# The split of x moved ahead of the sums of z and B in a fused convolution and expert kernel

## What is computed

```python
# x (32, 64, 1024), cond_128 (32, 128), A_w (512, 1024), B_w (1024, 512)
h = conv1d(x, weight, pad=4, groups=4) + (cond @ c_weight.T)[:, :, None] + bias[None, :, None]
q = einsum('bsd,rd->bsr', h, Wq_w)               # 16 numbers a position
scores = einsum('bsr,er->bse', q, keys)          # 64 experts
top_vals, top_idx = top_k(scores, 16)
gate = scatter(softmax(top_vals), top_idx)       # 64 weights, 16 of them not 0
z = einsum('bsd,nd->bsn', h, A_w)                # 512 = 64 experts x rank 8
z_gated = (z.reshape(.., 64, 8) * gate[..., None]).reshape(.., 512)
out = x + 2.0 * einsum('bsn,on->bso', z_gated, B_w)
```

## Time and profile before

| | us |
|---|---|
| median of 3 runs (lowest, highest) | 250.67 (249.34, 251.91) |
| the profiled execution's own time | 250.78 |
| its span, first to last instruction | 249.0 |
| mean granted clock of TensorE | 0.966 of full |

### The profile page before, as it was taken

The page is one execution under the profiler, slowest core; times in us unless marked ns, Lnnn a source line. Parts: engine busy times, 40 slices in busy tenths (PEclk is TensorE's granted clock), DMA queues, the critical chain, the costliest instruction groups (busy, mean ns, idle before and its releaser), DMA issues.

```text
span 249.0 us, 4043 instructions
## 1 busy us (share of the span) xinstructions
PE 231.8 (93%) x1345; PEld 204.0 (82%) x1345; DVE 198.7 (80%) x449; ACT 128.9 (52%) x322; POOL 7.5 (3%) x16
## 2 busy tenths in 40 slices
PE   8999999999999959589998899979999799999995
PEld 6999998987889848478887789859898588998885
DVE  2799989999898995886978799894989747786642
ACT  5896685573646643276463664356651663333110
POOL 2010160000000000000000000000000000000000
PEclk9999999999999988959999999998999889999999
DMA  7994165879546252520744328270382413628552
GB/s 226 380 396 172 41 229 171 282 231 287 201 117 224 75 180 84 138 77 0 206 174 126 132 78 279 79 238 7 111 288 62 134 42 76 219 63 287 148 220 90
DMA packets 24869, 40.89 MB, mean 164 GB/s; under 512 B 2832, under 2 KB 11920, under 8 KB 24848
## 3 DMA queue, kind: packets, MB, share of 16 engines
q1 hardware_dynamic: 24704, 40.55, 50.3%
q10 hardware_dynamic: 144, 0.08, 0.2%
HBM read 28.04 MB, written 12.58 MB: 163 GB/s over the span
## 4 chain that ended last, share of the span: by engine, by line
PE 50%; DVE 36%; issue 9%; ACT 3%; DVEq 0%; POOL 0%; ACTq 0%; POOLq 0%
PE p_z L888 22%; DVE x_lo L1095 6%; DVE h_t L1137 5%; PE p_conv L837 5%; ACT x_hi L509 3%; DVE a_raw L1266 2%; DVE h_lo L1095 2%; DVE x_blk L1119 2%; PE p_out L929 2%; PE p_out L937 2%; PE p_out L930 2%; DVE a_lo L1095 2%; PE p_out L957 2%; PE p_out L961 2%; PE p_out L959 2%
## 5 line engine op out<-in xcount | busy, mean ns | idle before, releaser
L888 PE MATMUL p_z<-a_hi,h_lo 128*128 128x264 f32 x240 | 37.0, 301 | 0.0
L888 PEld LDWEIGHTS p_z<-a_hi,h_hi 128*128 128x128 f32 x240 | 34.8, 200 | 2.1 <-issue 0.4
L888 PE MATMUL p_z<-a_hi,h_hi 128*128 128x264 f32 x240 | 36.3, 297 | 0.0
L888 PE MATMUL p_z<-a_lo,h_hi 128*128 128x264 f32 x240 | 35.4, 292 | 0.0
L888 PEld LDWEIGHTS p_z<-a_hi,h_lo 128*128 128x128 f32 x240 | 34.1, 205 | 0.0
L888 PEld LDWEIGHTS p_z<-a_lo,h_hi 128*128 128x128 f32 x240 | 32.7, 197 | 0.0
L1095 DVE TENSOR_TENSOR x_lo<-x_blk,x_hi 128x1536 fp32r<-128x1536 f32 (+4 forms) x18 | 25.6, 1424 | 3.8 <-ACT x_hi L509 3.7
L559 ACT ACTIVATE p_conv<-p_conv,u 128x128 f32<-128x128 f32 x88 | 23.7, 357 | 1.7 <-PE p_conv L837 1.4
L509 ACT ACTIVATE h_hi<-h_t 128x1024 fp32r<-128x1024 f32 x16 | 17.0, 1060 | 13.9 <-DVE h_t L1137 13.9
L509 ACT ACTIVATE x_hi<-x_blk 128x1536 fp32r<-128x1536 f32 (+4 forms) x18 | 22.1, 1226 | 2.0 <-DVE x_blk L1119 1.1
L1095 DVE TENSOR_TENSOR h_lo<-h_t,h_hi 128x1024 fp32r<-128x1024 f32 x16 | 19.1, 1193 | 0.0
(11 more groups left out here) (160 smaller groups left out, 451.3 us busy)
## 6 DMA issues: line engine op xcount, KB each, us to landing
x_nat<-in_x_rows SPq DMA_DIRECT2D x16, 512.0 KB, 4.9
out_dram<-x_nat SPq DMA_DIRECT2D x31, 256.0 KB, 3.3
x_blk<-in_x_blocks SPq DMA_DIRECT2D x14, 516.0 KB, 3.7
z_dram<-a_raw SPq DMA_DIRECT2D x64, 64.0 KB, 1.8
a_raw<-z_dram SPq DMA_DIRECT2D x16, 256.0 KB, 3.0
a_raw<-in_a_wq SPq DMA_DIRECT2D x8, 264.0 KB, 6.2
x_nat<-in_b_w SPq DMA_DIRECT2D x4, 512.0 KB, 9.3
a_raw<-in_b_w SPq DMA_DIRECT2D x3, 512.0 KB, 3.7
```

Of the source, the lines that this page charges most:

```text
L888: mm = nc.tensor.matmul(z_bank(t, b)[:, 0:HB], h[:, t % 2, r, :], a[:, r, b * HB:(b + 1) * HB], start=k == 0 and r == 0, stop=k == 2 and r ...
```

## The change

Only the order of calls on ScalarE and VectorE is changed; no operation, wait or transfer is added or removed.

On VectorE `split_x(i + 3)` stands directly behind `turn_z(i)`, ahead of the turn of h. The two halves of the turn and split of q are moved among the sums: in even iterations from 6 on the turn of q stands behind `sum_z2`, the split of q behind `sum_z4`, and `split_h` and `split_z12` follow behind that. In odd iterations the turn of q stands behind `add_11`, then `split_h` and the split of q. In iteration 14 the turn and split of the last q stand at the end.

On ScalarE `split_x(i + 3)` stands directly behind the exponential and the copies of PSUM banks, ahead of the splits of z; `split_h(i + 2)` stands ahead of `split_z34`, `split_z22` and `split_z12`.

```diff
--- before.py
+++ after.py
@@ -739,22 +739,22 @@
                     copy_xy(m)
                 if i == NT - 2:
                     copy_xy(NP - 1)
+                if i + 3 < NT:
+                    split_x(i + 3)
                 if i <= FP:
                     split_z(i - 1)
                 if i == FP + 1:
                     split_z1(0)
-                if i >= FP + 2 and i % 2 == 0:
-                    split_z12((i - FP - 2) // 2)
-                if FP + 3 <= i < NT - 1 and i % 2:
-                    split_z34(m)
-                    split_z22(m)
-                if i + 3 < NT:
-                    split_x(i + 3)
                 if i in (5, 7):
                     split_w(i // 2)
                     sum_w(i // 2)
                 if i + 2 < NT:
                     split_h(i + 2)
+                if FP + 3 <= i < NT - 1 and i % 2:
+                    split_z34(m)
+                    split_z22(m)
+                if i >= FP + 2 and i % 2 == 0:
+                    split_z12((i - FP - 2) // 2)
                 if TB <= i < TB + 4:
                     split_bt(i - TB)
                 if FP + 3 <= i < NT - 1 and i % 2:
@@ -1430,45 +1432,46 @@
                     split_z1(0)
                 if TB <= i < TB + 4:
                     sum_b(i - TB)
+                if FP + 3 <= i < NT - 1 and i % 2:
+                    add_5(m)
+                    split_z34(m)
+                    split_z22(m)
+                    add_11(m)
                 if i == FP + 2:
                     sum_z31(0)
                     add(FP - 1, 1)
                     sum_z2(0)
-                    sum_z4(0)
                 elif i >= FP + 4 and i % 2 == 0:
                     sum_z31(m + 1)
                     add_12(m)
                     sum_z2(m + 1)
+                if i in (4, 6):
+                    sum_w(i // 2)
+                if TS <= i + 1 < NT - 1:
+                    turn_q(i + 1)
+                if i == FP + 2:
+                    sum_z4(0)
+                elif i >= FP + 4 and i % 2 == 0:
                     add_22(m)
                     sum_z4(m + 1)
-                elif FP + 3 <= i < NT - 1:
-                    add_5(m)
-                    split_z34(m)
-                    split_z22(m)
-                    add_11(m)
+                elif i + 2 < NT:
+                    split_h(i + 2)
+                if TS <= i + 1 < NT - 1:
+                    split_q(i + 1)
                 if i >= FP + 2 and i % 2 == 0:
+                    if i + 2 < NT:
+                        split_h(i + 2)
                     split_z12((i - FP - 2) // 2)
-                if i + 3 < NT:
-                    split_x(i + 3)
-                if i in (4, 6):
-                    sum_w(i // 2)
-                if i == NT - 2:
-                    split_z34(NP - 1)
-                if TS <= i + 1 < NT:
-                    turn_q(i + 1)
-                if i < NT - 3:
-                    split_h(i + 2)
-                if TS <= i + 1 < NT:
-                    split_q(i + 1)
-                if i == NT - 3:
-                    split_h(i + 2)
                 if TB <= i < TB + 4:
                     split_bt(i - TB)
                 if FP + 3 <= i < NT - 1 and i % 2:
                     split_z1(m + 1)
                 if i == NT - 2:
+                    split_z34(NP - 1)
                     split_z22(NP - 1)
                     add_21(NP - 2)
+                    turn_q(NT - 1)
+                    split_q(NT - 1)
             add_5(NP - 1)
             add_11(NP - 1)
             split_z(NT - 2)
```

## The result

| | before | after |
|---|---|---|
| median, us | 251.19 | 240.70 |
| lowest, highest of 4 runs | 249.34, 251.91 | 240.40, 240.79 |
| profiled execution, its span | 250.78, 249.0 | 240.40, 238.6 |
| mean granted clock | 0.966 | 1.0 |

The ratio is 0.9591, with a 95% interval of 0.9535 to 0.9647: 10.5 us less.

The account below looks back on a forecast made before the run. TensorE, busy 231.8 of 249.0 us, was taken as the bound, waiting 13.4 us for x in conv_sum, with VectorE's queries' chain taking over. Gains 2.3 + 8.8, less 1.2 for the clock, took 250.8 to 240.8 us; range 235.5 to 246.

Parts of the forecast that it names:

- Tiles 3 to 5, no gain and a new wait: VectorE waits 1.3, 1.0, 1.3 us ahead of the turn of q; tile 6's scores copy comes at 96.0, about 0.35 late.
- Tiles 6 and 7: New 1.5 us wait in tile 6; VectorE copies tile 7's scores at 112.0; gain by tile 8's scores matmul 2.3 us.
- s(7): Start of TensorE's scores matmul of tile 7, forecast at 109.6 us instead of 113.19.
- Even tiles: Tiles 8, 10, 12: scores matmul to next in 12.3 us; 0.85 us wait for q; 1.0 us cover for conv_sum.
- Odd tiles: Tiles 9, 11: 14.45 us between scores matmuls against TensorE's own 13.7, a 0.75 us wait; tile 13 12.95.
- The clock: TensorE's wait of about 3 us ahead of tile 7's scores matmul lowers its clock; 1.2 us charged.
- The sum: Whole kernel: 2.3 + 8.8 - 1.2 = 9.9 us gained on the profiled execution's 250.8, giving 240.8 us.
- slower: Rival, chance 0.05: queries' chain already bounds the kernel, so new waits in tiles 3 to 6 add 5.1 us: 255.9.
- No change: Rival, chance 0.05: the turn of h comes as late as x_lo did, conv_sum waits as before: 250 us.
- The clock falls as often as before: Rival, chance 0.13: remaining waits start low-clock stretches, 1.5 us in three places, 4 us in all: 244.8.
- tighter chain: Rival, chance 0.14: VectorE and the queries' chain need half a microsecond more in each of eleven tiles: 246.3 us.
- More is won: Rival, chance 0.13: new waits in tiles 3 to 6 hidden, clock stays up, odd tiles keep 13.7: 234.6 us.

Follow-up runs that it names:

- e4: Changed kernel with the sum of B moved earlier on VectorE in tiles 3 to 5, and its rounding earlier on ScalarE in tile 6; 236.60 us.
- e7: Changed kernel with one more 128x512 transpose on VectorE ahead of the turn of z in tiles 7 to 12; 244.22 us.
- e1: Kernel before with split_x alone moved, on both engines, to where the change has it; 243.13 us, ratio 0.9696.
- e6: Changed kernel with three more 512-column matmuls on TensorE in conv_sum of tiles 7 to 12; 240.90 us.
- e3: Kernel before with split_x moved on ScalarE only; 245.02 us, ratio 0.9743.
- e8: Kernel before with its waits for x kept but filled with 42 unneeded TensorE matmuls in tiles 5, 6, 8, 10 and 12; 244.21 us, ratio 0.9771.
- e5: e4 plus two VectorE moves: add_22 ahead of the turn of q in even tiles, add_11 ahead of the split of z34 in odd ones; 234.55 us.

## Why the prediction was right, step by step

240.8 us was forecast and 240.70 measured, so the size of each term matters more than the sum. Two terms missed in opposite directions.

- *Tiles 3 to 5, no gain and a new wait.* The waits were put at 1.3, 1.0 and 1.3 us and measured 1.21, 1.01 and 1.21; the copy of the scores of tile 6 was put at 96.0 and came at 96.26. e4 shows their cause. The idle 0.5 us ahead of a MAX8 in tile 5, of which 0.35 was counted as won, came again (0.52).
- *Tiles 6 and 7.* The wait of 1.5 us was 1.53; sc(7) 112.0 against 112.09, s(7) 109.6 against 109.73, s(8) 124.9 against 125.09. TensorE's wait of about 3 us ahead of s(7) came in two pieces, 0.59 in conv_sum and 2.19 ahead of the scores matmul.
- *Even tiles.* 12.3 forecast, 12.33 measured, with the wait ahead of the turn of q at 0.84 for 0.85. conv_sum waited for the turn of h in no tile from 7 on; the cover of 1.0 us held, and held in e7, too, with 0.64 us less of it. In tile 6 it did not: 0.59 us. The prediction had called a wait of conv_sum for the turn of h a sign of being wrong, and it had named neither this one nor the 1.38 us for the new conv weights in tile 5. Neither moved the end: the scores matmuls behind them waited another 2.19 and 2.07 us for the chain over VectorE.
- *Odd tiles.* The 13.7 us that TensorE needs by itself are the 13.71 of e1. 14.45 forecast, 14.59 measured; tile 13 12.95 against 13.06. These make up most of the 0.5 us by which the gain from s(8) to s(14) was over-estimated (8.8 forecast; (214.80 - 127.24) - (204.32 - 125.09) = 8.3 measured).
- *The clock.* This step failed. I took off 1.2 us for a fall behind the wait ahead of s(7). That wait came, 2.19 us long, and the clock stayed at 1.00 in the profiled execution. In the execution at 0.993 it may have fallen (it has no trace), and its time is the same within 0.4 us: VectorE is then the later engine, as e6 shows with 4.1 us of added matmuls that cost 0.2 by the medians. With a longer wait at the same place, 3.83 us in e1, the step holds: there the clock fell and the scores of tile 8 came 1.3 us later.
- *The sum.* The profiled execution gained 250.78 - 240.40 = 10.4 us against 9.9: the missing charge of 1.2, less 0.6 from the terms above, less 0.1 behind s(14), a stretch that I held unchanged.

What I had not separated is what the gain is made of. The sums went from the start of one scores matmul to that of another, and the old lengths, 17.83 and 16.14 us, held the slow clock. That is why the total came out. But the text spoke of 13.4 us of waiting, and e3 and e8 show that about half of the 10.5 us (5.8 in e8, 4.8 to 6.7 by its interval) is matmuls at the low clock behind these waits. Where I reasoned by waits alone, in e3's expectation, I missed by 3.3 us.

Of the rivals, "slower" is refuted by the time. Its new waits did come (1.21, 1.01, 1.21 and 1.53, 5.0 us in all), and VectorE's idle ahead of the scores copies in the earlier trace rows (0.45, 0.21, 1.97 and 2.24, 4.9 us) is gone in their place. What added VectorE work costs in the kernel before was not run; e7 shows only that it costs nearly its full length behind the change. "No change" failed as conv_sum never waits for x, and waits for the turn of h in one tile alone. "The clock falls as often as before" and "tighter chain" didn't happen. "More is won" is what e4 and e5 reach by other edits: 3.5 us for the waits of tiles 3 to 6 were foreseen there, and e4 got 4.1.

## What to carry to other kernels

When a late operation is moved ahead in a program-ordered queue, list what it used to cover: here 1.68 us of VectorE work had hidden ScalarE's rounding and take of q, and four new waits of 1.0 to 1.5 us took their place. Moving the producer earlier as well took three of them away and left 0.58 us of the fourth. Measure a stage from one start of the same matmul to the next, since that holds the wait and the slow clock behind it. Then ask which engine is later at each meeting point: added work on the other one tells it at once (4.1 us on TensorE, busy for 94% of the span, cost 0.2, and 3.8 us on VectorE, busy for 83%, cost 3.5).

## What the runs showed of the hardware

The same tile with waits of 1.86 us kept the clock at 1.00 (tile 8) and lost it (tile 10, 0.89), and with a wait of 1.47 us (e3) it was kept in both. After the change waits of 2.07 and 2.19 us, one tile apart, left it at 1.00; in e1 a wait of 3.83 us ahead of the scores of tile 7 was followed by 0.89. Matmuls put into a wait kept the clock at 1.00 in tiles 5, 8 and 10, not in tile 6 (0.90), and cost nothing: 42 of them took 5.8 us off the kernel before. That kernel's spread of 4 us looks like noise of the measurement, but it goes with the granted clock, 0.959 to 0.978, and the changed kernel spreads over 0.4 us.
